# A decoder layer on one core: the value bank is copied out by VectorE in front of max 3, not by ScalarE behind exponential 3

## What is computed

```
scores = jnp.einsum('cbqh,cbkh->cbqk', q, k) / scale     # scale = sqrt(16)
attn = jax.nn.softmax(scores, axis=-1)
o = jnp.einsum('cbqk,cbkh->cbqh', attn, v)
```

## Time and profile before

| | us |
|---|---|
| median of 2 runs | 2055.75 (2055.62 to 2055.88) |
| profiled execution | 2056.88 |
| its span, first to last instruction | 2055.2 |
| PE busy | 2012.4 (98%) |
| DVE busy | 1640.6 (80%) |
| ACT busy | 1327.8 (65%) |
| POOL busy | 488.4 (24%) |

### The profile page before, as it was taken

The page is one execution under the profiler, slowest core; times in us unless marked ns, Lnnn a source line. Parts: engine busy times, 40 slices in busy tenths (PEclk is TensorE's granted clock), DMA queues, the critical chain, the costliest instruction groups (busy, mean ns, idle before and its releaser), DMA issues.

```text
span 2055.2 us, 43093 instructions
## 1 busy us (share of the span) xinstructions
PE 2012.4 (98%) x12800; PEld 1150.8 (56%) x12800; DVE 1640.6 (80%) x1727; ACT 1327.8 (65%) x2429; POOL 488.4 (24%) x878
## 2 busy tenths in 40 slices
PE   9999999999999999999999999999999999989996
PEld 4788876444444444444444444444444487767774
DVE  4433357999999999999999999999999467886777
ACT  0111114888888888888888888888888633453344
POOL 0000001122112212221221122122212452574245
PEclk9999999999999999999999999999999999999997
DMA  5465736467676576765775766757667679763672
GB/s 189 133 174 149 182 113 124 78 140 144 104 135 139 107 138 127 118 137 101 139 144 102 131 138 107 138 120 120 138 108 207 214 246 335 270 233 135 226 263 92
DMA packets 214416, 315.28 MB, mean 153 GB/s; under 512 B 105424, under 2 KB 121808, under 8 KB 202064
## 3 DMA queue, kind: packets, MB, share of 16 engines
q1 hardware_dynamic: 214352, 314.47, 63.8%
HBM read 211.06 MB, written 101.19 MB: 152 GB/s over the span
## 4 chain that ended last, share of the span: by engine, by line
PE 90%; DVE 6%; ACT 2%; POOL 1%; issue 1%; DMA 0%; DVEq 0%; POOLq 0%; SPq 0%; ACTq 0%
PE psum L187 24%; PE psum L562 23%; PE psum L589 15%; PE psum L224 13%; PE psum L600 11%; PE psum L88 2%; DVE stats L1527 1%; PE psum L1447 1%; DVE y L1652 1%; ACT probs L739 1%; DVE gates L1626 1%; DVE gates L1623 1%; ACT gates L1376 1%; DVE y L1557 1%; DVE gates L1645 0%
## 5 line engine op out<-in xcount | busy, mean ns | idle before, releaser
L231 DVE TENSOR_REDUCE neg_max<-psum 128x1 f32<-128x1024 f32 x1024 | 1191.0, 1216 | 97.4 <-PE psum L224 81.5
L739 ACT ACTIVATE probs<-psum 128x512 f32<-128x512 f32 x2048 | 1071.1, 600 | 189.5 <-PE psum L562 183.4
L562 PE MATMUL psum<-q_op,k_op 50*128 50x512 f32 x2048 | 658.1, 453 | 0.1
L224 PE MATMUL psum<-k_op,q_op 48*128 48x512 f32 x2048 | 614.1, 485 | 0.0
L562 PEld LDWEIGHTS psum<-q_op,k_op 50*128 50x128 f32 x2048 | 309.0, 190 | 447.1 <-ACT probs L739 441.0
L224 PEld LDWEIGHTS psum<-k_op,q_op 48*128 48x128 f32 x2048 | 387.6, 315 | 25.5 <-DVE neg_max L231 8.2
L589 PE MATMUL psum<-probs,v_op 128*32 128x512 f32 x2560 | 340.9, 604 | 3.8 <-ACT out L728 0.7
L187 PE MATMUL psum<-x_wino,conv_w 128*128 128x512 f32 x1152 | 275.6, 395 | 0.0
L600 PE MATMUL psum<-probs,v_op 128*32 128x256 f32 x3072 | 245.4, 391 | 0.5 <-ACT probs L739 0.5
L187 PEld LDWEIGHTS psum<-x_wino,conv_w 128*128 128x128 f32 x1152 | 214.6, 188 | 45.6
L242 POOL CAST neg_max_parts<-neg_max 128x8 fp32r<-128x8 f32 x128 | 24.5, 192 | 721.5 <-DVE neg_max L231 721.5
(11 more groups left out here) (106 smaller groups left out, 1699.4 us busy)
## 6 DMA issues: line engine op xcount, KB each, us to landing
q_op<-qk_parts_dram SPq DMA_DIRECT2D x384, 128.0 KB, 4.9
conv_w<-conv_w_parts_dram SPq DMA_DIRECT2D x32, 1536.0 KB, 6.7
qk_parts_dram<-qk_parts SPq DMA_DIRECT2D x128, 256.0 KB, 3.1
k_op<-qk_parts_dram SPq DMA_DIRECT2D x384, 64.0 KB, 5.2
conv_w_parts_dram<-conv_w_parts SPq DMA_DIRECT2D x16, 1536.0 KB, 7.0
attended_dram<-out SPq DMA_DIRECT2D x64, 256.0 KB, 3.6
attended_parts_dram<-o_parts SPq DMA_DIRECT2D x128, 128.0 KB, 3.3
gates<-in_ctx_dram SPq DMA_DIRECT2D x32, 512.0 KB, 7.5
```

The source lines that it names most:

```text
L224: return nc.tensor.matmul(mem["pair"][t % 2][:, lane * HALF:(lane + 1) * HALF], ops["q"][i][r, b, t:S:QT], ops["k"][i][r, b, :], start=Tru ...
L231: nc.vector.tensor_reduce(ops["max"][b][:, t:t + 1], mem["pair"][t % 2][:], AX_X, ALU.max, negate=True).then_inc(ops["maxed"], 1)
L562: nc.tensor.matmul(score_bank(k, t, last), kop[k][r, j // 2, n // 2 * P:(n // 2 + 1) * P], qop[k][r, j // 2, j % 2 * HALF:(j % 2 + 1) * HALF],
L739: nc.scalar.activation(probs[n % DEEP][:, c ^ n % 2, :], score_bank(k, t, last), ACT.Exp, scale=SCALE).then_inc(exp_done, 1)
```

## The change

The copy moves from ScalarE's queue to VectorE's. In a slot it stands in front of max 3 (behind max 2) instead of behind exponential 3. The waits are the same two, and the copy still signals `pv_out`. In the last slots, where VectorE has no maxima left, slot 62's copy stands behind the last reciprocal and in front of three preparations of operands for the last stage (`tern`, `wo_hi`, `wo_lo`), and slot 63's behind them.

```
-    EVACUATE_AFTER = 3
+    EVACUATE_AT = 3
...
-            def evacuate(s, k, uses):
-
-                act.wait_ge(pv_step, s * STEPS + STEPS + DEEP)
-                act.wait_ge(u_stored[k % 2], uses * DMA + DMA)
-                nc.scalar.copy(u[k % 2][:], pv_bank).then_inc(pv_out, 1)
-
...
-                            if t == EVACUATE_AFTER and not (first and k == 0):
-                                evacuate(s - 1, (k - 1) % 4, it * 2 + (k - 1) // 2)
...
-            evacuate(LAST * 4 + 3, 3, LAST * 2 + 1)
...
         @block.vector
         def _(dve):
+            def evacuate(s, k, uses):
+
+                dve.wait_ge(pv_step, s * STEPS + STEPS + DEEP)
+                dve.wait_ge(u_stored[k % 2], uses * DMA + DMA)
+                nc.vector.tensor_copy(u[k % 2][:], pv_bank).then_inc(pv_out, 1)
+
             def slot(it, k, first=False, units=16):
                 s = it * 4 + k
                 for n in range(units):
                     if n % QT == 0:
 
                         dve.wait_ge(split, s * 2 + n // QT + 2)
+                    if n == EVACUATE_AT and not (first and k == 0):
+                        evacuate(s - 1, (k - 1) % 4, it * 2 + (k - 1) // 2)
                     if n == 2 and k % 2 == 1 and not (first and k == 1):
                         recips(dve, nc, norm, it * 2 + (k - 3) // 2)
...
             recips(dve, nc, norm, PAIRS - 2)
+            evacuate(LAST * 4 + 2, 2, LAST * 2 + 1)
             dve.wait_ge(late["tern_in"], DMA)
...
                 .then_inc(late["wo_made"], 1)
+            evacuate(LAST * 4 + 3, 3, LAST * 2 + 1)
```

## The result

The changed kernel takes 2111.56 us (2111.45 to 2111.68) against 2055.75 before: a ratio of 1.0271, interval 1.0254 to 1.0287, so 2.7% slower. The forecast was 2111. Its profiled execution has a span of 2110.0 us, 54.8 more than before.

What follows compares the result with a forecast made beforehand. TensorE was taken to set the pace, one slot in 20.2 us. V0's delays, 62 / 4 x 3.59, less 0.5 us at the ends, gave 55.1 us on 2055.75: about 2111 us, range 2085 to 2119.

Steps and rivals of the forecast that it cites:

- The copy's length: VectorE's copy of the 128x512 value bank takes 0.69 us; 0.587 from below, 0.75 from above.
- Where VectorE reaches it: VectorE's queue reaches the copy behind max 2, the maximum of unit 2, when max 3 starts now, without idle.
- V0's delay: V0, a slot's first value matmul writing the bank again, waits for the copy: 0.90 us per slot.
- No recovery: Later in the slot nothing of the delay returns; VectorE's idle before max 4 grows from 0.49 to about 0.9 us.
- ScalarE's relief at nothing: ScalarE, losing the copy, gets 0.83 us per slot; costed at nothing, bound 13 us from shorter TensorE waits for exponentials.
- The rival "VectorE has room": The copy hides in VectorE's 0.49 us idle before max 4: 2056 us, or 2043 with ScalarE's relief; chance 0.08.
- The clock: Rival: TensorE, 4% idle in the attention stage, is granted 0.97 instead of 1.00; some 38 us more, 2149; chance 0.05.
- The ends: In the last slots, slot 62's copy, with VectorE idle before it, gains 0.5 us; the last copy is priced at 0.
- the cost of a late max 3: Max 3, unit 3's maximum, is 0.61 us late; U5, unit 5, waits for it but is later still behind V0.

Runs made afterwards that it cites:

- The turned order: Changed kernel with S7 (shifted scores) and U4 (a unit) in front of V0: 1.0075, 2070.40 us; same order on the kernel before: 1.0096, 2075.30 us.
- the load alone: Kernel before, ScalarE still copying; VectorE adds two operands in front of max 3, which nobody waits for: ratio 1.0062.

## Why the prediction was right, point by point

- *The copy's length*: 0.69 us, taken from one row of line 153. The 64 copies took 0.673 to 0.692 us, median 0.679. The estimate of 0.66 by the Trainium skill ("VectorE: DVE Perf Modes", section on the TRN2 errata) was a little low.
- *Where VectorE reaches it*: right behind max 2, with no idle, in all four positions. With a copy of 0.17 us this arrival still costs 25 us.
- *V0's delay*: 0.76, 1.00, 0.83 and 1.00 us for k = 0 to 3, 0.90 on average, were the sum. TensorE's idle in front of V0 in the four slots shown is 0.72, 1.07, 0.86 and 1.06 us, where it was 0.08 at most before. Over all slots it grew by 0.87 us on average, and the slots from 20.24 to 21.13 us. So the mechanism was right slot by slot, not only in the sum.
- *No recovery*: VectorE's idle in front of max 4 went from 0.49 to 0.89 us, as worked out, and the later stalls kept their size. The turned order shows the other side: with U4 in front of V0 VectorE does catch up, and some 40 of the 56 us come back (ratio 1.0271 to 1.0075).
- *ScalarE's relief at nothing*: right in this order of TensorE's work: the idle in front of the value products grew by 53.6 us and the span by 54.8, so no gain stands against it. The shorter copy on ScalarE saved 6 us, less than the 13 I allowed, and part of that is V0's earlier start. In the turned order the relief is worth some 5 us.
- *The rival "VectorE has room"*: it has, nearly: the load alone costs 0.6%, and its trace shows U5's wait for max 3, not a lack of time. But room is not what V0 waits for. The Trainium skill ("Perfetto Trace Analysis", section Optimizing Scalar/DVE Operations) makes offloading from VectorE depend on whether it is saturated. That points the right way here, yet the loss came back in full with ScalarE as the copying engine, so saturation is not its cause.
- *The clock*: the granted clock stayed at 1.00 through the attention stage with TensorE 4% idle. The rival by the rule in "TensorE: Matmul & The Clock Gate", Part 1, of the Trainium skill did not happen; no run here shows how much idle it takes.
- *The ends*: slot 62's copy was to win 0.5 us. From the start of V7 to V0 it was 2.37 us before, and 1663.33 - 1661.38 = 1.95 after. It is 0.42. The 0.10 us from the copy to V0 was taken from a slot with k = 0, while slot 63 has k = 3; that it came out at 0.12 and not at 0.24 was luck.

Mis-sized, without consequence for the result: the cost of a late max 3. The prediction had it covered by V0's delay, which holds for the change; but in the runs without that delay it stood open. U5's weight load waited 0.40 us with the load and 0.55 with the copy in front of max 2, and the slots grew by 0.11 and 0.40 us on average (of the 0.40, 0.10 were V0's idle). The run with the load came out above what I expected.

## What to carry to other kernels

When work moves to another engine, ask first when that engine's queue reaches it, and only then how busy the engine is: the price is the lateness of what waits for the result, and everything in the waiting engine's queue behind it. Look for the engine's idle time in front of the moved step, not behind it; 0.49 us of idle one instruction too late hid nothing. If a wait must be late, put work of the waiting engine in front of it, above all the work that feeds the engine it waits for.

## What was not expected

The order of two waits on one instruction changes the time even where one of them is long over: in three slots of four TensorE started 0.24 us behind the copy with the late wait in front of the other, 0.15 behind it the other way round. With k = 0, where V0 has one wait more, it is 0.10 us before and after the change, and 0.15 with the waits turned. The further wait can't be the whole reason: in the changed kernel's last turn of the loop, which is written out, V0 follows by 0.10 us with k = 1 and 2 as well (slots 61 and 62: copies to 1624.43 and 1645.49, V0 at 1624.54 and 1645.59). Why it is shorter there stays open. And the releaser in a row is only a name: the same hole in front of V0 stands under VectorE's copy, GpSimd's copy of the values, ScalarE's exponentials or "issue", from slot to slot.
